# A gated two-expert feed-forward layer: the expert's last row of second-layer tiles one turn later

## What is computed

```
def _gated_ffn(x, wi0, wi1, wo):
    g = jax.nn.gelu(x @ wi0, approximate=True)
    l = x @ wi1
    return g * l @ wo
share_out = _gated_ffn(hidden_states, sWi0, sWi1, sWo)      # 512 -> 2048 -> 512
wi0, wi1, wo = Wi0[type_label], Wi1[type_label], Wo[type_label]
expert_out = the same with the item's own wi0, wi1, wo
gate_in = jnp.concatenate([expert_out[:, 0], share_out[:, 0]], axis=-1)
weights = jax.nn.softmax(jax.nn.relu(gate_in @ g0) @ g1, axis=-1)
out = x + expert_out * weights[:, 0] + share_out * weights[:, 1]
```

## Time and profile before

| | |
|---|---|
| three runs, median | 1995.35 us (1992.99, 1995.35, 1995.88) |
| profiled execution, its own time | 1992.22 us |
| span from its first to its last instruction | 1990.4 us |
| granted TensorE clock, mean | 0.996 |
| busy: TensorE (PE) | 1963.4 us, 99% |
| busy: weight loads (PEld) | 1731.1 us, 87% |
| busy: VectorE (DVE) | 1525.8 us, 77% |
| busy: ScalarE (ACT) | 1037.1 us, 52% |
| busy: GpSimd (POOL) | 78.3 us, 4% |
| DMA | 194.83 MB, mean 98 GB/s |

### The profile page before, as it was taken

How to read it: one execution, slowest core, us unless ns; L and a number is a source line. 1 busy time by engine, 2 the same in 40 slices (tenths; PEclk the granted TensorE clock), 3 DMA queues, 4 the chain that set the end, 5 groups by cost and what they waited for, 6 DMA issues and landing times.

```text
span 1990.4 us, 29016 instructions
## 1 busy us (share of the span) xinstructions
PE 1963.4 (99%) x11158; PEld 1731.1 (87%) x11158; DVE 1525.8 (77%) x1819; ACT 1037.1 (52%) x1370; POOL 78.3 (4%) x56
## 2 busy tenths in 40 slices
PE   9999999999999999999999999999999999999997
PEld 8997888899998788889999888889999988888997
DVE  7776667789887766778988767668898966766886
ACT  6564444466566444446666544344666654444463
POOL 0010000001000000000101000000010100000000
PEclk9999999999999999999999999999999999999999
DMA  4431111245452111124444221112444421111342
GB/s 159 138 106 48 48 60 52 64 144 160 138 174 92 53 59 48 54 79 145 151 150 161 80 64 53 53 54 86 153 144 138 159 90 48 55 57 48 107 159 85
DMA packets 152412, 194.83 MB, mean 98 GB/s; under 512 B 10450, under 2 KB 116946, under 8 KB 150482
## 3 DMA queue, kind: packets, MB, share of 16 engines
q1 hardware_dynamic: 152274, 192.98, 30.6%
HBM read 184.55 MB, written 8.39 MB: 97 GB/s over the span
## 4 chain that ended last, share of the span: by engine, by line
PE 96%; DVE 2%; issue 0%; ACT 0%; DMA 0%; SPq 0%; DVEq 0%; POOL 0%; POOLq 0%; ACTq 0%
PE ps_out L415 35%; PE ps_pv L396 18%; PE ps_pv L406 17%; PE ps_c L396 13%; PE ps_c L406 13%; DVE al L807 1%; DMA a_src<-experts 0%; DVE act L1038 0%; SPq L270 0%; ACT ah L585 0%; DVE lin L903 0%; DVE lin L899 0%; DVE a_src L826 0%; ACT ps_c L699 0%; DVE s_out L1128 0%
## 5 line engine op out<-in xcount | busy, mean ns | idle before, releaser
L807 DVE TENSOR_TENSOR al<-a_src,ah 128x512 fp32r<-128x512 f32 (+2 forms) x289 | 400.8, 1388 | 37.0 <-ACT ah L585 35.2
L585 ACT CAST ah<-a_src 128x2048 fp32r<-128x2048 f32 (+2 forms) x285 | 336.7, 1193 | 3.2 <-DVE a_src L826 3.2
L396 PE MATMUL ps_pv<-xh,al 128*128 128x256 f32 x1024 | 290.1, 283 | 0.1
L396 PE MATMUL ps_pv<-xl,ah 128*128 128x256 f32 x1024 | 289.8, 283 | 0.0
L396 PE MATMUL ps_pv<-xh,ah 128*128 128x256 f32 x1024 | 289.8, 283 | 0.0
L629 ACT ACTIVATE act<-ps_c 128x256 f32<-128x256 f32 (+1 forms) x192 | 87.5, 456 | 313.8 <-PE ps_c L396 173.5
L396 PE MATMUL ps_c<-xh,al 128*128 128x256 f32 x772 | 218.9, 284 | 2.3 <-DVE al L807 2.3
L396 PE MATMUL ps_c<-xh,ah 128*128 128x256 f32 x772 | 219.1, 284 | 0.0
L396 PE MATMUL ps_c<-xl,ah 128*128 128x256 f32 x772 | 219.1, 284 | 0.0
L684 ACT COPY ps_pv<-ps_c 128x512 f32<-128x512 f32 x127 | 72.4, 570 | 280.7 <-PE ps_c L406 193.8
L415 PE MATMUL ps_out<-wo0h,hidl 128*128 128x512 f32 x512 | 199.7, 390 | 0.8 <-DVE wo0l L807 0.8
(11 more groups left out here) (95 smaller groups left out, 3919.0 us busy)
## 6 DMA issues: line engine op xcount, KB each, us to landing
a_src<-experts SPq DMA_DIRECT2D x256, 256.0 KB, 3.8
raw_wo<-experts SPq DMA_DIRECT2D x128, 256.0 KB, 2.8
a_src<-shared SPq DMA_DIRECT2D x128, 256.0 KB, 3.0
g_sb<-g_rows SPq DMA_DIRECT2D x16, 1024.0 KB, 5.5
raw_wo<-shared SPq DMA_DIRECT2D x64, 256.0 KB, 2.8
x_src<-x_cols SPq DMA_DIRECT2D x32, 256.0 KB, 3.9
g_sb<-x_rows SPq DMA_DIRECT2D x7, 1024.0 KB, 4.9
out<-s_out SPq DMA_DIRECT2D x7, 1024.0 KB, 7.5
```

The lines of the kernel that those rows point to most:

```text
L396: mm = nc.tensor.matmul(ps[:, a * HALF:(a + 1) * HALF], a_op[ap][:, i, a, k, :], x_op[xp][:, j, k, h, :], start=(start and a == 0 and k == ...
L585: nc.scalar.copy(a_op[HI][:, i:j, :, :, :], a_src[m % 2][:, i:j, :, :, :]).then_inc(a_hi_done, 1)
L807: nc.vector.tensor_tensor(to, of, hi.bitcast(F32), ALU.subtract).then_inc(done, 1)
```

## The change

Turn 8 (the first gate turn of a pair) loses the four expert tiles, turn 9 (the first linear turn) gets them, with the waits for `hid_ready` and `wo_ready` of that step. On ScalarE the four copies out move from the end of `shared_gate` to the end of `shared_lin`, behind the two `a_hi`. The two counting functions follow. It happens once in each of the four pairs; no instruction is added or dropped.

```diff
 def down_turn(n):
-    return last_turn(n + 1) if is_wide(n) else first_turn(n + 1)
+    return last_turn(n + 1)
@@
 def downs(t):
-    return 4 * t - (4 if WIDE0 < t % PAIR_TURNS < EXPERT1 else 0)
+    return 4 * t - (4 if WIDE0 <= t % PAIR_TURNS < EXPERT1 else 0)
@@ shared_turn (TensorE)
-                if a == GATE:
+                if a == (GATE if c > 0 else LIN):
                     pe.wait_ge(hid_ready, n)
                     pe.wait_ge(wo_ready, n)
                 for m in range(MC):
                     if c > 0:
                         shared_tile(m, a, b, n - 1)
-                    elif a == GATE:
+                    elif a == LIN:
                         expert_tile(m, b, n - 1)
@@ shared_gate, shared_lin (ScalarE)
                 wo_hi(n)
-                if c == 0:
-                    copies_out(b, t)
-            def shared_lin(n):
+            def shared_lin(n, c, b):
@@
                 a_hi(n + 1, 0)
                 a_hi(n + 1, 1)
+                if c == 0:
+                    copies_out(b, t)
```

More of the change, by code:

```diff
@@ L790, in shared_pass @@
                     shared_gate(n0 + c, c, b)
-                    shared_lin(n0 + c)
+                    shared_lin(n0 + c, c, b)
             first_step()
```

## The result

The changed kernel takes 1979.72 us (median of four runs, 1979.53 to 1980.06), the one before 1994.8 us beside it (1992.99 to 1995.88). The ratio is 0.9926, interval 0.9908 to 0.9943: faster by 15 us. The profiled execution took 1979.53 us, its span 1977.8; for the one before it was 1992.22 and 1990.4.

The account below looks back on a forecast made before the run. TensorE, busy 1963.4 of 1990.4 us, bounds the kernel. 1992.22 − 14.44 for waits before turn 10 + 0.5 for P6 gives 1978.3; a third of the 3.1 us offset makes 1979.5 us, own range 1976.5 to 1983, asked range to 1984.

Parts of the forecast that it names:

- The wait in front of turn 10: TensorE waits for `a_lo` group 0 before P1 of turn 10; all goes, 4.72 + 3 × 3.24 = 14.44 us.
- P6 of turn 9 is late next: P6's weight load waits for ScalarE's `copy_p1`: 0.1 to 0.15 us late per pair, 0.4 in the fourth; 0.5 taken.
- P4, P1 and P5 free: After turn 8 loses its tiles, these products of turns 8 and 9 find their inputs ready; no loss.
- the copies and SyncE at no cost: Moved copies in turn 9 push nothing, cost 0 (bounds 0 and 0.3); SyncE issues weights 5.4 us earlier, cost 0.
- The sum: Whole kernel, profiled execution: 1992.22 − 14.44 + 0.5 = 1978.3 us.
- The offset: Median of runs lies 3.1 us above the profiled execution; a third taken as staying, giving 1979.5 us.
- The price of a slow stretch: TensorE at 1.2 GHz after the first pair's wait before turn 10: 1.48 us.
- The bound of 5.9 us for the spread: Kernel before: slow clock on none to all four waits before turn 10 spreads its time over 5.9 us.
- The larger wait at P6: Rival: the wait moves to P6 of turn 9, 4.8 us in place of 0.5, about 1983.8 us; chance 0.08.
- A stall by `wo_hi`: Rival: in turn 8, late `raw_wo` holds `copy_p1` behind `wo_hi`; at 5 us each, 1999.5 us; chance 0.03.
- Tiles that don't cover: Rival: in turn 9 `a_hi` or `a_lo` stands behind the copies out; nothing won, 1995 us; chance 0.02.

Follow-up runs that it names:

- The longer queue: Changed kernel plus one more 1024-column ScalarE copy ahead of `wo_hi` in turn 8 of each pair; 1982.66 us, ratio 0.9934.
- the longer queue under a tile: Changed kernel with one expert tile left in turn 8, plus an extra 1024-column ScalarE copy ahead of `wo_hi` there; 1977.76 us, ratio 0.9908.
- the repeated run: The changed kernel measured again without further change, on the same chip beside others; 1979.68 us, ratio 0.9917.

## Why the prediction was right

- *The wait in front of turn 10.* Right in place, mechanism and size: 14.44 us by the blocks. `a_lo` group 0 was to be 2.1 us early; its end 2.29 us after 152.91, at 155.20, is 2.2 us ahead of the weight load that needs it, and both `a_lo` were done at 156.33, before P4 of turn 9 ended. One to three moved tiles gave the line that this step implies.
- *P6 of turn 9 is late next.* Right: 0.05 us in three pairs for the 0.1 to 0.15 taken, 0.36 in the fourth for 0.4; 0.51 in all, for the 0.5 in the sum. The prediction's own terms add up to 0.7 to 0.85, and it took less without sizing the deduction, so that the total came out so closely is partly luck. The weight load was 0.11 us late by the trace, and the matmul behind it lost less than that. The longer queue, and the longer queue under a tile, show the mechanism.
- *P4, P1 and P5 free, the copies and SyncE at no cost.* No wait of TensorE for them is left. One reading was off without effect: turn 10's first tile comes 9 us after the copies (165.91 against 157.02), not 13. The next load of `a_src` began while SyncE moved nothing else, and the landing times of the page are the same (3.0 us for `a_src` from `shared`).
- *The sum.* 14.44 − 0.5 = 13.94 was forecast; the profiled executions show 13.94 between their first and last blocks. The 1978.3 us for the profiled execution was 1.2 too low, because the start took 1.27 us longer in this one. I had left the start out of the sum and only in the range.
- *The offset.* Here the forecast's 1979.5 was near the 1979.72 partly by luck. I let a third of the 3.1 us offset stay, as a guess between two readings. The runs say that it goes wholly, as far as they can tell: the median of the changed kernel is 0.2 us from its own profiled execution, and 3.7 us left the median of the kernel before when its waits were filled. What made up for it in the forecast was the start, 1.27 us longer. The price of a slow stretch was mis-sized: 1.48 us in the one seen, up to 2.8 where the wait is 3.4 us long. The bound of 5.9 us for the spread was also too small for the 7.0 us that ten runs then showed. Longer slow stretches or the start, which differs by 2.3 us between traces, can each make up the difference; which it was isn't shown.
- *The rivals.* The larger wait at P6 needed another 1 us on ScalarE, as the longer queue shows. A stall by `wo_hi` was not there: it starts at 143.16, straight behind the GELU in place (142.20, 1.06 us). Tiles that don't cover: that is just what happens when the copies stand ahead of `a_hi`, and worse than the 1995 us given for it, for 2001.38 were measured. The rival was priced without the clock: the waits alone, 15.2 us in all, would give 1994.9.

The gain from median to median, 15.9 us beside the repeated run (1995.57 to 1979.68), is 13.0 of waiting (four times 3.24), plus 3.7 of slow clock, less 0.6 at P6: 16.1. The 3.7 is itself a difference of medians, so the agreement tests the other terms and no more.

## What to carry to other kernels

When TensorE is 99% busy, look for turns that lack a block of work which depends on nothing new, and lay their shortfall against the spare cover of their neighbour: here 3.3 us were missing in one turn while the turn before had 5.4 to spare and, with all of it gone, was late by at most 0.5. Move only as much as the late side needs, since the giver gets a limit of its own; three tiles of four closed both gaps. What is moved along on the other engines must go behind whatever feeds the next wait: the same tiles with their copies two instructions further ahead made the kernel slower.

## What the hardware showed beyond that

- A wait of TensorE has a second price. Behind 3.4 us without a matmul the clock went to 1.2 GHz each time (four of four), for 1.3 to 2.8 us of loss; behind 2.9 us one time in four in each of three traces, always in the first pair; behind 1.6 us never in four. With matmuls on zeros in the gap it stayed at 2.4 GHz in all four places of the one trace.
- A profiled execution can be a lucky one: three of the kernel before took 1992.2 to 1992.8 us, while the medians of its runs were 1994.8 to 1996.1.
- In the fourth pair the in-place GELU of turn 8 starts 0.27 us late against `c12`, in the kernel before as in the changed one. With the extra ScalarE copy, which stands behind this GELU but in each of the three pairs ahead of it too, the delay is gone in both traces. Its cause stays open.
